# DLRM tower: the gram products of a tile in two halves with other products between them, a tenth table by one-hot products, and gathers in slots of four tables

## The reference, cut to what matters

```python
e = jnp.stack([tbl_f[ids[:, f]] for f in range(26)], axis=1)   # 2048 x 26 x 128, float32
sd = jnp.einsum('bfd,bd->bf', e, dense)
ss = jnp.einsum('bfd,bgd->bfg', e, e)
z = jnp.concatenate([dense, sd, ss[:, iu, ju]], axis=1)        # iu, ju: pairs with i < j
h = jnp.concatenate([z, dense], axis=1)                        # 2048 x 607
h = jnp.maximum(h @ W_top1 + b_top1, 0.0)                      # 512
h = jnp.maximum(h @ W_top2 + b_top2, 0.0)                      # 256
y = h @ W_top3                                                 # 2048 x 1
```

## Time and profile before

| what | us |
|---|---|
| median of three runs | 394.25 (394.03, 394.25, 397.19) |
| the profiled execution's own time | 390.34 |
| its span, from the first to the last instruction | 388.5 |
| PE busy, of the span | 325.2 |
| POOL busy | 263.9 |
| DVE busy | 223.5 |
| ACT busy | 188.1 |

### The profile page before, as it was taken

The page is one execution under the profiler, slowest core; times in us unless marked ns, Lnnn a source line. Parts: engine busy times, 40 slices in busy tenths (PEclk is TensorE's granted clock), DMA queues, the critical chain, the costliest instruction groups (busy, mean ns, idle before and its releaser), DMA issues.

```text
span 388.5 us, 14097 instructions
## 1 busy us (share of the span) xinstructions
PE 325.2 (84%) x6128; PEld 300.9 (77%) x6128; DVE 223.5 (58%) x655; ACT 188.1 (48%) x282; POOL 263.9 (68%) x283
## 2 busy tenths in 40 slices
PE   0875888877989898989899798979899798987756
PEld 0765786767989797978799698968799697977745
DVE  1999869645854694557467385547466574503011
ACT  2346563714655464536445464535455463546122
POOL 5777677777777777777777777777777777760020
PEclk9999899955999999999999899998999998999699
DMA  7998633554345443653264434543265435420130
GB/s 177 241 243 247 199 86 76 128 140 105 92 108 128 122 109 72 146 138 82 79 146 136 96 88 104 136 115 84 80 142 141 102 79 113 122 58 3 33 84 0
DMA packets 44639, 44.48 MB, mean 114 GB/s; under 512 B 28738, under 2 KB 34326, under 8 KB 44577
## 3 DMA queue, kind: packets, MB, share of 16 engines
q1 hardware_dynamic: 34350, 25.23, 26.8%
q0 software_dynamic: 8832, 18.00, 18.3%
q10 hardware_dynamic: 1394, 0.35, 0.4%
HBM read 38.01 MB, written 5.55 MB: 112 GB/s over the span
## 4 chain that ended last, share of the span: by engine, by line
PE 70%; DVE 10%; issue 9%; DMA 7%; ACT 3%; SPq 1%; ACTq 0%; DVEq 0%
PE et_ps L528 30%; PE g_ps L547 14%; PE m_ps L504 12%; PE et_ps L520 7%; DVE one_hot L444 7%; PE m_ps L571 5%; DMA et<-tbl_in 4%; PE m_ps L580 1%; DMA gram_rows<-gram 1%; DMA idb<-ids_one_hot 1%; DVE table_lo L433 1%; ACT et L367 1%; DMA zt_raw<-gram_rows 1%; DVE w_lo L429 1%; DVE w_hi L427 1%
## 5 line engine op out<-in xcount | busy, mean ns | idle before, releaser
L325 POOL DMA_INDIRECT rows<-tbl_in,idx x272 | 260.8, 959 | 86.4 <-issue 77.2
L444 DVE TENSOR_SCALAR one_hot<-idb,first_row 125x256 fp32r<-125x256 int32 x576 | 181.5, 385 | 73.5 <-PE et_ps L528 39.5
L528 PE MATMUL et_ps<-one_hot,table_hi 125*128 125x256 f32 x576 | 156.5, 306 | 21.5 <-DVE one_hot L444 17.6
L528 PE MATMUL et_ps<-one_hot,table_lo 125*128 125x256 f32 x576 | 148.3, 291 | 0.0
L528 PEld LDWEIGHTS et_ps<-one_hot,table_hi 125*128 125x128 f32 x576 | 115.1, 200 | 27.2 <-issue 15.9
L528 PEld LDWEIGHTS et_ps<-one_hot,table_lo 125*128 125x128 f32 x576 | 115.4, 200 | 0.1
L367 ACT COPY et<-et_ps 128x384 f32<-128x384 f32 (+1 forms) x80 | 86.5, 1085 | 41.7 <-PE et_ps L520 39.9
L547 PE MATMUL g_ps<-et 128*27 128x26 f32 x4096 | 58.6, 196 | 29.7 <-issue 22.1
L547 PEld LDWEIGHTS g_ps<-et 128*27 128x27 f32 x4096 | 47.9, 107 | 41.3 <-issue 34.5
L359 ACT COPY et<-et_ps 128x256 f32<-128x256 f32 (+1 forms) x80 | 44.3, 675 | 39.4 <-PE et_ps L528 39.4
L380 ACT COPY gram<-g_ps 128x416 f32<-128x416 f32 x32 | 28.5, 889 | 66.6 <-PE g_ps L547 66.6
(11 more groups left out here) (44 smaller groups left out, 215.8 us busy)
## 6 DMA issues: line engine op xcount, KB each, us to landing
idb<-ids_one_hot SPq DMA_DIRECT2D x32, 256.0 KB
gram_rows<-gram SPq DMA_DIRECT2D x30, 169.0 KB
rows<-tbl_in,idx POOLq DMA_INDIRECT x272
et<-tbl_in SPq DMA_DIRECT2D x6, 448.0 KB
xt<-dense_t SPq DMA_DIRECT2D x8, 128.0 KB
idb<-ids_one_hot SPq DMA_DIRECT2D x8, 128.0 KB
raw<-tbl_in SPq DMA_DIRECT2D x2, 448.0 KB
zt_raw<-gram_rows SPq DMA_DIRECT2D x15, 48.0 KB
```

Of the source, the lines that this page charges most:

```text
L325: nc.gpsimd.indirect_dma_start(out=rows[:, i % ROW_RING, n, :], out_offset=None, in_=tables[GATHERED[k]], in_offset=bass.IndirectOffsetOnA ...
L444: nc.vector.tensor_scalar(one_hot[0:KP, at % OH_RING, :], idb[0:KP, pair % ID_RING, n % 2, :], first_row[0:KP, 0:1], float(k), ALU.subtrac ...
L528: last = nc.tensor.matmul(ps[:, n % 2 * CH:(n % 2 + 1) * CH], part[0:KP, n, k, :], one_hot[0:KP, at % OH_RING, :], start=k == 0 and part i ...
```

## The change

The lists of steps are written anew, a tenth table (17) goes from the gathered to the one-hot tables, the sixteen tables left are gathered in four slots of four a tile, and to make room in SBUF for the tenth table the one-hot ring, the staging buffers and `raw` become smaller. The weights' raw copies move to other buffers, are loaded later and are split at G0 to G3 of chunk 0. The whole diff:

```diff
@@ -7,7 +7,7 @@
 B, F, D = 2048, 26, 128
 H1, H2 = 512, 256
 NPAIR = F * (F - 1) // 2
-ONE_HOT = (1, 3, 4, 5, 6, 10, 12, 14, 16)
+ONE_HOT = (1, 3, 4, 5, 6, 10, 12, 14, 16, 17)
 ROWS = 1000
 GATHERED = tuple(f for f in range(F) if f not in ONE_HOT)
 NO, NG = len(ONE_HOT), len(GATHERED)
@@ -29,14 +29,14 @@
 
 
 PHASE = (
-    "O4 Z0 Z1 G4 G5 G6 G7 X0 Z2 W0 T0 O5 K0 T1 D0 D1 O6 K1 D2 D3 T2 D4 D5 O7 K2 T3 D6 D7 D8 O8 T4 M0 G0 "
-    "G1 G2 G3 T5 O0 T6 Y0 O1 T7 O2 T8 O3 T9").split()
+    "O5 Z0 Z1 G4 G5 X0 G6 G7 Z2 W0 O6 T0 K0 D0 D1 O7 T1 D2 D3 K1 O8 D4 D5 T2 D6 D7 D8 O9 T3 K2 G0 G1 O0 "
+    "M0 G2 G3 T4 O1 Y0 T5 O2 O3 T6 O4 T7").split()
 LAST = (
-    "O4 Z0 Z1 G4 G5 G6 G7 X0 Z2 W0 T0 O5 K0 T1 D0 D1 O6 K1 D2 D3 T2 D4 D5 O7 K2 T3 D6 D7 D8 O8 T4 M0 G0 "
-    "G1 G2 G3 T5 Y0 T6 z0 z1 x0 k0 z2 T7 k1 k2 T8 T9").split()
+    "O5 Z0 Z1 G4 G5 X0 G6 G7 Z2 W0 O6 T0 K0 D0 D1 O7 T1 D2 D3 K1 O8 D4 D5 T2 D6 D7 D8 O9 T3 K2 G0 G1 T4 "
+    "M0 G2 G3 Y0 T5 z0 z1 x0 k0 z2 T6 k1 k2 m0 T7 y0").split()
 TAIL = (
-    "G4 G5 G6 G7 W0 M0 Y0 D0 D1 D2 D3 D4 D5 D6 D7 D8 x0 z0 k0 z1 k1 z2 k2 m0 y0").split()
-AHEAD = 4
+    "G4 G5 x0 G6 G7 W0 D0 D1 D2 D3 D4 D5 D6 D7 D8 z0 k0 z1 k1 z2 k2 m0 y0").split()
+AHEAD = 5
 
 LAST_WRITES, LAST_READS = ("SSAA", "SPSPSPSPS")
 G_STEPS = 8
@@ -54,7 +54,7 @@
         for step in (PHASE if p < NCH - 1 else LAST if p < NCH else TAIL)
         if 0 <= p + later(step[0], int(step[1:])) < NCH]
 
-SIZES = (4, 4, 3, 3, 3)
+SIZES = (4, 4, 4, 4)
 FIELD_AT = list(accumulate(SIZES, initial=0))
 TR_TABLES = max(SIZES)
 TR_HALF = len(SIZES)
@@ -63,9 +63,9 @@
 G_BANKS = 4
 G_GROUPS = GROUPS // G_BANKS
 ID_RING = 2
-OH_RING = 14
+OH_RING = 12
 ROW_RING = 6
-STAGES = 6
+STAGES = 5
 
 
 def ends_pair(n):
@@ -156,14 +156,14 @@
 
 
         spare = et[:, (ET_TILES - 1) * TILE_W:]
-        raw = sb("raw", [128, 2560])
+        raw = sb("raw", [128, 1024])
         W = KT * D
-        staging = [spare[:, i * W:(i + 1) * W] for i in range(3)] + [raw[:, 0:W], raw[:, W:2 * W], gram[:, 0:W]]
+        staging = [spare[:, i * W:(i + 1) * W] for i in range(3)] + [raw[:, 0:W], gram[:, 0:W]]
         table = [staging[n % STAGES].rearrange("p (k d) -> p k d", k=KT) for n in range(NO)]
         flat_h2, flat_z = [t[:, :, :].rearrange("p a b -> p (a b)") for t in (h2, zt_raw)]
-        w1_raw = [flat_h2, flat_z[:, 0:H1], raw[:, 0:H1], raw[:, H1:2 * H1]]
-        w1_again = raw[:, 2 * H1:3 * H1]
-        w2_raw = raw[:, 3 * H1:5 * H1]
+        w1_raw = [flat_h2, flat_z[:, 0:H1], raw[:, 0:H1], spare[:, W:W + H1]]
+        w1_again = raw[:, H1:2 * H1]
+        w2_raw = spare[:, 0:W]
 
         w1_parts = [sb(f"w1_{part}", [128, 1 + KZ, H1], f32r) for part in ("hi", "lo")]
         w2_parts = [sb(f"w2_{part}", [128, H1 // 128, H2], f32r) for part in ("hi", "lo")]
@@ -284,7 +284,7 @@
             loaded = PAIRS
             sp.dma_start(idx[:, first:], ids_gather[:, first:]).then_inc(idx_in[1], 16)
             load_dense(1)
-            sp.wait_ge(table_lo_done, 5)
+            sp.wait_ge(table_lo_done, 9)
             sp.dma_start(w1_raw[0], w1_dense[0:D, :]).then_inc(w_in[0], 16)
             sp.dma_start(w1_again, w1_dense[D:, :]).then_inc(w_in[0], 16)
             for k in range(KZ):
@@ -345,6 +345,7 @@
                     wait(act, g_done, (c - 1) * G_BANKS + G_BANKS // 2)
                     if c == 1:
                         act.wait_ge(table_lo_done, NO)
+                        act.wait_ge(w_ready, W_READY)
                     act.wait_ge(xt_in[c % 2], (c // 2 + 1) * 16)
                     for t in range(TILES):
                         last = nc.scalar.copy(et_fields(TILES * c + t, F, 1)[:, 0, :].rearrange("d (q g) -> d q g", q=4),
@@ -475,8 +476,9 @@
             for kind, c, n in PLAN:
                 if kind == "O" and c * NO + n + 1 < NCH * NO:
                     build(c * NO + n + 1)
-                    if c == 1 and n < KZ + 2:
-                        split_weights(n)
+                if kind == "G" and c == 0 and n < 4:
+                    for k in ((0, 1), (2,), (3,), (4,))[n]:
+                        split_weights(k)
                 if kind == "G" and c == 0 and n == G_STEPS - 1:
                     split_x(0)
                 if kind == "Z":
```

## The result

The changed kernel takes 413.42 us (median of four runs, 411.02 to 413.96) against 395.72 for the kernel before in the same comparison (394.03 to 400.54): a ratio of 1.045, 95% interval 1.037 to 1.053. It is slower, and outside the range given. The profiled execution's span is 411.3 us against 388.5.

A forecast was written before the change was run, and what follows sets the result against it. PE was taken to bound the kernel, with POOL nearly level. Start to 88.7, first full phase 37.2, five phases to 331.2 and the end gave 385.2 us of span, 3.3 under 388.5: 391.0 us (-0.8%), range 384.5 to 399.

The forecast's parts named there:

- The queue of SP: Id loads at new places in SP's queue; the one at O7 is wanted a third of a phase later: cost nothing.
- The stops: PE's stops in G are instruction fetches, up to 2.0 us each; cutting G leaves 0.5 us a phase (bounds 0 and 1.5).
- The third rival: The stops in G are not fetches and stay, and the added O is paid: about +12, 406 us; chance 0.08.
- The sign that I gave: Mark in the profile after: PE's "issue" idle in G falls under a third of before.
- The phase: One phase between two G0: 38.5 + 1.66 + 0.5 + 0.4 = 41.06 us, 1.97 less than 43.03.
- POOL did not bound: Rival that POOL's gathers were the bound, so the phase falls with them, to 40.2 at least: 386 us; chance 0.05.
- The start: Up to G0 of chunk 1: O5 ends at 72.2, G0 comes at 88.7 us, 4.1 later than before (bounds 0 and +9).
- Rival 1: The start costs nothing and the stops in G vanish: 385.8 us; chance 0.17.
- rival 2: PE runs at half clock in the start and becomes slower than DVE: +7.4 there, 398.4 us; chance 0.20.
- The first full phase: G0 of chunk 1 to G0 of chunk 2, without Y and M0: 37.2 us against 43.4, ending at 125.9.
- The last phase: Last of the five phases before G0 of chunk 7: counted like the others at 41.06 us, with 0.5 of stop.
- The end: From G0 of chunk 7: 27.8 us to 359.0, then a 23.9 tail plus 2.3 for half clock, to 385.2.

The follow-up runs named there:

- experiment 2: Changed kernel with the load of the dense rows moved in SP's order from O7 to K2: 396.65 us (1.010 of the kernel before).
- experiment 4: Kernel before, nine tables, with only the lists changed to cut both G halves (X0 between G5 and G6, M0 between G1 and G2): 385.33 us, 0.980.
- experiment 5: Kernel before with 128 semaphore increments put ahead of PE's first product: 394.15 us (one run).
- experiment 7: Kernel of experiment 2 with the G halves whole again and K2 ahead of O9: 411.02 us beside 396.34 for the kernel before, 1.037.
- experiment 3: Changed kernel with both moves: dense load to K2, and D0 and D1 behind O7: 398.93 us (1.013 of the kernel before).
- experiment 8: Kernel of experiment 2 with the kernel before's order at the end (m0, y0, x0 behind G7): 396.32 us (1.010).

## Why the prediction was wrong, step by step

- **The queue of SP: the step that failed.** The prediction says of the queue "I cost it at nothing", and gives no reason for the load that mattered. I followed the id loads through the queue, and took the one of O7 as wanted a third of a phase later. I did not follow the dense load right behind it. It waits for a split that DVE does at K2; the new lists put K2 behind O9 and T3 instead of right behind O7, and DVE builds O0's one-hots ahead of it, with ids from the same queue. Phases of 44.7 us instead of 41.06 came of it. Moving this one load gives 16 to 17 of the 22.4 us between 413.4 and the 391.0 forecast. The wait that I did look at, for the ids of O7, is still 4.7 to 5.5 us a phase in experiment 2 and costs PE nothing.
- **The stops.** Right in cause, and shown by experiments 4, 5 and 7. The cut is worth 9 to 12 us. The third rival is out, and with it the "mostly hidden" of the Trainium skill. The sign that I gave, issue idle under a third of before, fails in the changed kernel (12.4 of 22.1) and holds with the load moved (6.0).
- **The phase.** Right once the load is moved: 41.0 to 42.2 in experiment 3, 41.6 on average, against 41.06. POOL did not bound the ten tables: it waited for PE 23.2 us, where it had waited 7.3.
- **The start.** Right: G4 of chunk 0 at 72.26 in the changed kernel (72.2 summed for the end of O5 just before it) and G0 of chunk 1 at 90.45 (88.7); in experiment 2 at 88.42. Rival 1 wanted it at 84.6 and rival 2 some 7 us after the forecast, so both are out.
- **The first full phase** was mis-sized: 37.2 summed, 38.8 in experiment 3 (91.08 to 129.91), 40.5 in the changed kernel (90.45 to 130.94). In experiment 2 G0 of chunk 1 is earlier and G0 of chunk 2 is not (88.42 and 129.49, 41.1). What holds G0 of chunk 2 was not tried.
- **The last phase** was mis-sized by 5: 342.44 - 296.28 = 46.2 in experiment 3, not 41.1. I took half a microsecond of stop for each phase, as a mean; but X0 has only 24 instructions, and in the last phase one block ends with X0 and the next is all G6 and G7 (of chunk 6). The two show in the changed kernel's chain as two stops in a row, 337.81 and 341.08:

```profile
336.18 1.63 PE m_ps L506 x12
337.81 1.51 issue
339.31 0.72 PE g_ps L549 x50
340.03 0.01 issue
340.05 0.75 PE g_ps L549 x34
340.79 0.07 issue
340.86 0.22 PE g_ps L549 x2
341.08 1.81 issue
```

  The O behind them takes 3.62 us for its 16 matmuls, at half clock. In experiment 3 the same two places of the program stop for 0.57 and 2.20 us:

```profile
322.63 1.65 PE L551 MATMUL g_ps<-et 128*27 128x26 f32 x128 [0.57 <-issue]
326.48 0.36 PE L532 MATMUL et_ps<-one_hot,table_hi 125*128 125x256 f32 x1 [2.20 <-DVE one_hot L447]
```

  The second is put down to DVE, but the eight one-hots of this O (O6) had all been built by 319.1, while a packet of the queue "instruction" is in at 325.10, 1.4 us before PE resumes: it is a fetch too. Behind it the granted clock is 0.69 from 326 to 331 us. How the 5 us divide between stops and clock was not measured apart.
- **The end.** Right in size: from G0 of chunk 7 to the copy of the last bank 26.9 us in experiment 3 (27.8 summed), and 395.5 - 369.3 = 26.2 from there on (26.2 summed). From their first to their last start K0 to K2 take 6.49 us there and 4.29 in the kernel before, so the half clock costs 2.2 (2.3 summed). That the missing M0, Y0 and x0 are its cause is not shown (experiment 8).

With both loads moved (experiment 3) the span is 395.5 us against 385.2 summed; 4 us of this are there by G0 of chunk 2 (129.91 against 125.9), 2 come in the next four phases and 5 in the last, and the end gives 1 back. So even the mended kernel is no faster than before. On one chip nine tables with the cut took 385.33 us (experiment 4) and ten 396.65 (experiment 2): the tenth table and what came with it cost what the cut gives back.

## What to carry to other kernels

When steps are put in a new order, follow every wait of each in-order queue, those of small transfers that seem to be early too, back to the engine that ends it, and ask which of this queue's other transfers that engine needs first: a ring of such waits costs each of its latencies once a phase. A stretch of very short instructions on PE should be broken by long ones at less than every 256 instructions, and by enough of them; cutting it by itself was worth 2% here. Spending PE's time to spare an engine that is not yet the bound takes the gain away again.

## What the runs showed of the hardware

- Instruction fetch is a cost of PE when 256 instructions take 1.9 us: stops of 0.7 to 2.7 us at most blocks wholly of 27-column matmuls (experiment 5 and the kernel before), and the place moves by the instructions put in front (239 to 175 matmuls for 128 instructions). Each such stop ends 1.1 to 1.6 us after a packet of the queue "instruction" is in.
- Such a stop can cost twice: after the two in a row in the changed kernel, the granted clock was 0.59 from 342.8 to 347 us and 16 matmuls took 3.62 us instead of 1.92.
- The profile can name the wrong cause for one: a stop of 2.20 us was put down to a one-hot that had been built 7 us earlier (experiment 3).
- The granted clock was 0.50 through the first matmuls after a gap of 3.2 us that followed real work (383 to 388 us in experiment 8, in a run that was slower than its others), and 0.65 over K0 to K2 after 11.7 us of idle (experiment 2); in the kernel before, after 2.7 us of idle, it was 1.00.
